# ViT layer with mixture of experts: weight parting, tile list and first gathers moved into the batch stage; own buffer for the second input

## The chip, the cores and the metric

One core of a Trainium2 chip runs the whole layer in one launch. The metric is the device time of that launch in microseconds (us); lower is better. PE is TensorE, ACT ScalarE, DVE VectorE, POOL GpSimd, SP SyncE, which here only issues DMAs.

## The reference, cut to what matters

```
h = attention(x)                           # 8 batches, 512 tokens, width 256, 16 heads
h = concatenate([cls_tok, h], axis=1)      # 513 rows a batch
h = h + ssm(layernorm(h))                  # h_t = W h_(t-1) + B u_t, y = C h + D u
u2 = layernorm(h)
shared = (silu(u2 @ Wg_s.T) * (u2 @ Wu_s.T)) @ Wd_s.T
probs = sigmoid(u2 @ Wr.T + rb); scores, idx = top_k(probs, 2)
out = shared + sum over e of cw[e] * (silu(u2 @ Wg[e].T) * (u2 @ Wu[e].T)) @ Wd[e].T   # 8 experts, inner width 512
return h + out
```

## The kernel before, in words

Four stages follow each other: stage_qkv, stage_attention, stage_mix, stage_experts. Each is a block in which every engine runs its own hand-written list of instructions, with semaphores between the engines. At the end of a block each engine drains and all five meet at a barrier (its rows have the line of the block, L782 for the mix stage, L1350 for the experts, L338 for attention).

**stage_mix** (from L779) goes through the 8 batches in 9 steps: `step(b, par, prev, this, nxt)` does batch b's recurrence (`this`), the shared expert of batch b-1 (`prev`) and the attention output and first normalisation of b+1 (`nxt`). In step b:

- DVE: `normalise(b, ..., 2)` writes the second input into `u`, the same buffer as the first input, `normalise(b + 1, h, 1)` overwrites it. Hence DVE waits for `u2_stored` (SP's store of u to HBM) before the latter (L1252). POOL makes the power (L873) that each `normalise` (L1166) needs. DVE also chooses the two experts of each row (`top_two`), computes their slots (`place`) and at the very end the list of tiles (`list_tiles`, L1324).
- POOL: in `step`, multiplies `ud`, adds `h2`, and scatters 8 times per batch (L900) the row number and weight of each row to its slot in `table` in HBM.
- SP: in `step`, loads the heads of b+1 (L845), loads one expert's weights (L856), stores the second input (L859) and the output rows of b-1 (L863), in that order.
- PE: turns rows by products with `ident` (L981), the recurrence's products (L993, L1049), the shared expert (L1011, L1019). ACT: SiLU and copies of turned tiles.

**Weight parting.** The expert products are exact to FP32 by three short products (`split_products`, L72) of parts: `short` (rounded weight, made by ACT in `shorten_weights`) and `rest` (weight minus short, `cut_weights`). There are 16 places of 128x1024 elements, n = 0 to 7 for wg, 8 to 15 for wu. `rest` lies over the loaded weights, `short` over buffers of the mix stage, so these must be dead first. DVE cuts 11 places (two in step 8, nine in the expert stage), POOL five (three after the last scatters, two after the first gathers). ACT rounds eight in step 8, eight in the expert stage.

**stage_experts** takes 72 tiles of 128 slots in a ring of 8. SP loads a tile's slots (`load_slot`: read the tile's number from `tile_i`, then a DMA), POOL gathers its rows of x (`gather`, L1397), PE turns them (L1434), DVE parts x (L1528, L1530), PE multiplies (L72), turns (L1453) and goes down (L1460), DVE weighs, POOL adds into the output by an indirect DMA (L1407). Before the loop: 8 slot loads, 4 gathers, the last 11 cuts.

The lines that set the order around the change:

```
dve.wait_ge(ev["u2_stored"], 16 * b + 16)          # L1252, ahead of normalise(b + 1, h, 1)
pool.wait_ge(ev["slots_out"], 16 * (2 + 2 * TT * B))   # end of POOL's mix list
pool.wait_ge(mem["acc_stored"], 16 * B)            # experts, ahead of the 4 first gathers
pe.wait_ge(mem["ev_cut"]["dve"], sum(map(len, DVE_CUTS)))
pe.wait_ge(mem["ev_cut"]["pool"], sum(map(len, POOL_CUTS)))   # ahead of the first expert product
```

## Time and profile before

| what | value |
|---|---|
| time, median of 3 runs | 1296.78 us (1296.37 to 1297.04) |
| the profiled execution's own time | 1293.25 us |
| its span, first to last instruction | 1291.2 us, 21179 instructions |
| busy: PE, DVE | 1179.1 us (91%), 832.4 us (64%) |
| busy: ACT, POOL | 496.1 us (38%), 404.7 us (31%) |
| mean granted TensorE clock | 0.962 of full speed |
| mix stage, expert stage | from about 522 to 886, and on to 1291 |

The busy time of an engine is the sum of its instructions' spans. In the timeline views a row gives the start, the duration, the engine (SPq is the queue of SP), the line, the operation with what it writes and reads, how many such instructions follow each other, and in brackets the idle time before it with what ended it. A stretch's row gives busy us and number of instructions per engine, then the granted clock of PE.

### The profile page before, as it was taken

To read this page: it belongs to the slowest core of one execution; us is meant where nothing else is said; L and a number is where in the kernel's file an instruction comes from. 1 tells how busy PE (TensorE), PEld (TensorE's weight loads), DVE (VectorE), ACT (ScalarE), POOL (GpSimd) and SP (SyncE) were. 2 spreads that over 40 slices of the span, in tenths; PEclk is the share of its full clock that TensorE was granted. 3 is DMA by queue.
4 is the path that set the end of the run, shared out by engine and by line. 5 is a ranking of instruction groups with operands and counts; after the bars stand their busy time and mean duration, and the time that the engine had idled before them with its cause. 6 is when DMAs were issued, how large, how long until landed. Compare 5 with 4: busy or idle time off the path is not lost. (4 is left out here: it accounts for less than half of the span.)

```text
span 1291.2 us, 21179 instructions
## 1 busy us (share of the span) xinstructions
PE 1179.1 (91%) x5606; PEld 704.0 (55%) x5607; DVE 832.4 (64%) x1458; ACT 496.1 (38%) x867; POOL 404.7 (31%) x520
## 2 busy tenths in 40 slices
PE   6996999999999999767999999982999999999996
PEld 3652233333333332454566665551888888888885
DVE  4998788888888883367777788856333433333332
ACT  2430777777777778211212121242122222222221
POOL 1021431101101110211444333446344554455443
PEclk9996999999999999878999999996999999999999
DMA  9885233333333321022334323311133333333332
GB/s 287 309 275 184 71 99 93 103 96 96 100 92 97 103 85 34 33 55 77 98 98 97 70 51 75 82 34 33 30 53 49 49 51 55 49 49 49 53 53 33
DMA packets 108674, 113.04 MB, mean 88 GB/s; under 512 B 26080, under 2 KB 97904, under 8 KB 107600
## 3 DMA queue, kind: packets, MB, share of 16 engines
q1 hardware_dynamic: 90528, 89.05, 24.0%
q0 software_dynamic: 18112, 23.57, 10.6%
q8 instruction: 17, 0.28, 0.1%
q14 instruction: 17, 0.14, 0.0%
HBM read 68.81 MB, written 43.62 MB: 87 GB/s over the span
## 5 line engine op out<-in xcount | busy, mean ns | idle before, releaser
L637 DVE TENSOR_REDUCE neg_max<-by_query 128x2 f32<-128x1024 f32 x256 | 301.3, 1219 | 62.5 <-PE by_query L538 61.7
L696 ACT ACTIVATE k_wu_e<-by_key 128x512 f32<-128x512 f32 x512 | 277.2, 600 | 83.5 <-PE by_key L546 80.0
L546 PE MATMUL by_key<-k_wg_e 99*128 99x512 bf16 x512 | 179.2, 384 | 3.8 <-ACT k_wu_e L696 2.1
L538 PE MATMUL by_query<-k_wg_e 96*128 96x512 bf16 x512 | 160.4, 396 | 11.3 <-PEq L106 7.5
L1407 POOL DMA_INDIRECT out_rows<-y,slot x72 | 113.2, 1572 | 182.9 <-DVE y L1544 179.9
L1500 ACT ACTIVATE gate<-ps_up 128x512 f32<-128x512 f32 x72 | 43.2, 600 | 304.4 <-PE ps_up L72 304.4
L1460 PE MATMUL ps_y<-k_wd_e,acts_T 128*128 x576 | 136.1, 379 | 0.8 <-ACT acts_T L1509 0.8
L557 PE MATMUL pv<-k_wu_e,k_wd_e 128*32 128x512 f32 x1024 | 136.2, 604 | 0.2 <-ACT k_wu_e L696 0.2
L546 PEld LDWEIGHTS by_key<-k_wg_e 99*128 99x128 bf16 x512 | 41.9, 97 | 145.3 <-ACT k_wu_e L696 84.6
L1460 PEld LDWEIGHTS ps_y<-k_wd_e,acts_T 128*128 128x128 f32 x576 | 109.1, 190 | 18.6 <-issue 1.0
L1528 DVE CAST x_T<-ps_x 128x256 fp32r<-128x256 f32 x72 | 30.6, 424 | 107.6 <-PE ps_x L1434 107.6
L451 POOL CAST k_max_parts<-neg_max 128x16 bf16<-128x16 f32 x32 | 6.1, 191 | 283.0 <-PE by_key L546 244.8
L538 PEld LDWEIGHTS by_query<-k_wg_e 96*128 96x128 bf16 x512 | 47.2, 99 | 84.6 <-DVE neg_max L637 13.8
L1544 DVE TENSOR_SCALAR y<-ps_y,slot 128x256 f32<-128x256 f32 x72 | 34.8, 483 | 78.0 <-DMA out_rows<-y,slot 51.6
L1397 POOL DMA_INDIRECT x_in<-kept_x_rows,slot x72 | 73.6, 1022 | 31.5 <-issue 21.6
L1537 DVE TENSOR_TENSOR acts<-gate,ps_up 128x512 f32<-128x512 f32 x72 | 49.5, 687 | 52.3 <-PE ps_up L72 52.3
L72 PE MATMUL ps_up<-wg_short,x_T 128*128 x144 | 71.1, 493 | 5.2 <-issue 5.2
L900 POOL DMA_INDIRECT kept_table<-k_pay,k_slot_i x64 | 63.2, 987 | 24.6 <-issue 18.4
L873 POOL TENSOR_TENSOR mix_rstd<-mix_mv,k_minus_half 128x4 f32<-128x4 f32 x16 | 16.4, 1027 | 171.5 <-DVE mix_mv L1161 171.3
L206 PE MATMUL qk_ps<-k_wu_e,k_wqkv 128*128 128x512 f32 x128 | 57.8, 605 | 12.3 <-DMA k_wu_e<-in_xT 12.3
L1011 PE MATMUL mix_pairs<-mix_u_T,k_wg_s 128*128 128x512 f32 x128 | 62.6, 612 | 1.3 <-DVE mix_act_T L1139 1.2
L72 PE MATMUL ps_up<-wu_short,x_T 128*128 x144 | 63.2, 439 | 0.0
(211 smaller groups left out, 1906.8 us busy)
## 6 DMA issues: line engine op xcount, KB each, us to landing
k_wg_e<-kept_qk SPq DMA_DIRECT2D x384, 64.0 KB, 2.2
kept_qk<-qk_parts SPq DMA_DIRECT2D x32, 384.0 KB, 3.4
kept_v<-v_ones SPq DMA_DIRECT2D x8, 1024.0 KB, 5.8
k_wd_e<-kept_v SPq DMA_DIRECT2D x32, 256.0 KB, 3.0
...
```

The source lines that it names most:

```text
L72: mm = pe.matmul(out, short(lhs[a]), short(rhs[b]), start=(start and n == 0), stop=(stop and n == 2))
L206: mm = pe.matmul(qk_ps[:, j, :], wqkv[:, c, j * P:(j + 1) * P], xt[:, par, c, :], start=(c == 0), stop=(c == DC - 1))
L538: pe.matmul(by_query[:, pair_bank(b, g, k // 2) + k % 2, :], q_rows[0:KROWS, g, h, t * P:(t + 1) * P], k_rows[0:KROWS, g, h, :], start=Tru ...
L546: pe.matmul(by_key[:, key_bank(job), :], k_rows[0:SROWS, g, h, kt * P:(kt + 1) * P], q_rows[0:SROWS, g, h, :], start=True, stop=True).then ...
L557: mm = pe.matmul(pv[VW * h:VW * (h + 1), :], v_unit[:, g, kt, h, :], probs[:, G * (kt // 2) + h, kt % 2, :], start=(kt == 0), stop=(kt == ...
L637: dve.tensor_reduce(neg_max[:, g % 2, 2 * n:2 * n + 2], by_query[:, bank:bank + 2, :], AX.X, ALU.max, negate=True).then_inc(query_read, 1)
L696: act.activation(probs[:, key_tile(j) // 2 * G + j // 2 % G, j % 2, :], by_key[:, key_bank(job), :], ACT.Exp, scale=float(HD) ** -0.5).the ...
L900: pool.indirect_dma_start(out=dram["table"], in_offset=None, in_=mem["pay"][:, t, n, :], out_offset=bass.IndirectOffsetOnAxis(ap=mem["slot ...
L1011: mm = pe.matmul(pairs[:, m % 2, n, :], w[:, c, m * P:(m + 1) * P], u2_T[:, c, :], start=(c == 0), stop=(c == DC - 1))
L1397: pool.indirect_dma_start(out=x_in[:, r % X, :], out_offset=None, in_=dram["x_rows"], in_offset=bass.IndirectOffsetOnAxis(ap=slot[:, r % R ...
L1407: pool.indirect_dma_start(out=dram["out"], in_=y[:, r % 2, :], in_offset=None, compute_op=ALU.add, out_offset=bass.IndirectOffsetOnAxis(ap ...
L1460: mm = pe.matmul(ps_y[:, r % 2, 0:D], acts_T[:, m, :], mem["wd_e"][:, bass.ds(e, 1), m, :], start=(m == 0), stop=(m == FC - 1))
```

## The change

1. **Second input in its own buffer.** `normalise(b, ..., 2)` writes `u2`, POOL and the turn of u keep `u`. `normalise(b + 1, h, 1)` waits for the turn of u (`u_turned`) instead of the store; `normalise(b, ..., 2)` waits for u2's turn and store of one batch ago.
2. **Places sorted by last use.** The mix buffers lie in the order in which they die, and `w_short` is one tensor with wg and wu of an expert side by side; place n is now expert n // 2, wg for even n. Places 0 and 1 lie on a piece of their own (`EARLY`).
3. **Parting by ACT and DVE alone.** ACT rounds 0 and 1 before step 0, 2 to 12 in step 7, 13 to 15 in step 8. DVE cuts 0 and 1 in step 0, 2 and 3 in step 7, 4 to 10 in step 8, 11 to 15 in the expert stage. POOL cuts none.
4. **Tile list, slots and gathers in the mix stage.** DVE lists the tiles right after placing the last batch; SP loads 4 slot tiles before the last output store and 4 after it; POOL gathers 4 tiles at the end of its mix list. Two of four scratch buffers of the mix stage (`back`) lie on `x_in`.
5. **SP's order.** An expert's weights are loaded after the store of u2 and for b + 1; expert 0's at the stage's start.

```
+def cut_weights(dve, mem, n):
+    w, rest = ((mem["wg_e"], mem["wg_rest"]), (mem["wu_e"], mem["wu_rest"]))[n % 2]
+    dve.wait_ge(mem["ev_cut"]["shortened"], n + 1)
+    dve.tensor_tensor(short(rest[:, n // 2, :, :]), w[:, n // 2, :, :], mem["w_short"][:, n // 2, n % 2, :, :],
+                      ALU.subtract).then_inc(mem["ev_cut"]["rest_made"], 1)
...
+def load_slot(sp, mem, dram, i, r):
+    q = sp.value_load(mem["tile_i"][0:1, 0, bass.ds(RING * i + r, 1)], min_val=0, max_val=SLOTS // P - 1)
+    sp.dma_start(mem["slot"][:, r, :], dram["table"][bass.ds(q * P, P), :]).then_inc(mem["slot_in"][r], 16)
...
@@ SP, step of the mix stage
                 if this:
-                    for name in ("wg_e", "wu_e", "wd_e"):
-                        sp.dma_start(mem[name][:, bass.ds(b, 1), :, :], dram[name][:, bass.ds(b, 1), :, :]
-                                     ).then_inc(mem["experts_in"], 16)
                     sp.wait_ge(ev["u2_done"], b + 1)
                     sp.dma_start(dram["x_rows"][bass.ds(T1 * b + 1, S), :].rearrange("(t p) n -> p t n", p=P),
-                                 u[:, :, :]).then_inc(ev["u2_stored"], 16)
+                                 u2[:, :, :]).then_inc(ev["u2_stored"], 16)
+                if nxt:
+                    load_expert(b + 1)
+                if not this:
+                    sp.wait_ge(mem["tiles_listed"], 1)
+                    sp.wait_ge(ev["slots_out"], 16 * (2 + 2 * TT * B))
+                    for r in range(FIRST_X):
+                        load_slot(sp, mem, dram, 0, r)
...
+            load_expert(0)
             batches(sp, step)
-            sp.wait_ge(ev["u2_stored"], 16 * B)
+            for r in range(FIRST_X, RING):
+                load_slot(sp, mem, dram, 0, r)
@@ POOL, step of the mix stage
                 if not this:
-                    for n in POOL_CUTS[0]:
-                        cut_weights(pool, mem, n).then_inc(mem["ev_cut"]["pool"], 1)
...
+                    pool.wait_ge(ev["u2_stored"], 16 * B)
+                    pool.wait_ge(ev["cls_stored"], 32)
+                    for r in range(FIRST_X):
+                        pool.wait_ge(mem["slot_in"][r], 16)
+                        pool.sem_inc(ev["scatter_begun"])
+                        gather_x(pool, mem, dram, r)
...
@@ ACT, step of the mix stage
+                if last:
+                    act.wait_ge(mem["experts_in"], 16 * 3 * E)
+                    shorten_weights(act, mem, 2)
+                    act.wait_ge(ev["out_made"], 2 * B)
+                    shorten_weights(act, mem, 3)
...
+                if last:
+                    act.wait_ge(ev["bu_made"], B)
+                    act.wait_ge(ev["ud_done"], 2 * B)
+                    for n in (4, 5, 6):
+                        shorten_weights(act, mem, n)
...
+                if last:
+                    act.wait_ge(ev["state_done"], B)
+                    shorten_weights(act, mem, 7)
+                    act.wait_ge(ev["y_made"], 2 * B)
+                    for n in range(8, 13):
+                        shorten_weights(act, mem, n)
...
@@ DVE, step of the mix stage
                     if not this:
+                        cut_weights(dve, mem, 4)
                         place(b - 1)
                     shared_act(b - 1, 1)
                     if not this:
-                        cut_weights(dve, mem, DVE_CUTS[0][0]).then_inc(mem["ev_cut"]["dve"], 1)
+                        dve.wait_ge(ev["counts_read"], b)
+                        list_tiles(dve, chain(dve, ev["tile_steps"], 0), mem, flat_backs)
+                if not prev:
+                    for n in range(EARLY):
+                        cut_weights(dve, mem, n)
...
                 if this:
+                    dve.wait_ge(ev["u2_turned"], b)
+                    dve.wait_ge(ev["u2_stored"], 16 * b)
                     normalise(b, h2[:, par, :, :], 2)
...
+                if this and not nxt:
+                    for n in (2, 3):
+                        cut_weights(dve, mem, n)
...
                 if nxt:
-                    dve.wait_ge(ev["u2_stored"], 16 * b + 16)
+                    dve.wait_ge(ev["u_turned"], b + 1)
                     normalise(b + 1, h, 1)
@@ experts: PE, DVE
-            pe.wait_ge(mem["ev_cut"]["dve"], sum(map(len, DVE_CUTS)))
-            pe.wait_ge(mem["ev_cut"]["pool"], sum(map(len, POOL_CUTS)))
+            pe.wait_ge(mem["ev_cut"]["rest_made"], 2 * E)
...
-            for n in DVE_CUTS[1]:
-                cut_weights(dve, mem, n).then_inc(mem["ev_cut"]["dve"], 1)
+            for n in range(11, 2 * E):
+                cut_weights(dve, mem, n)
```

How the instructions stand, at three places. First SP at the start of the mix stage and in step 0; `mix_h` and `k_mix_u` are the shared names of the tiles that lie in those places, among them h2 and u2. Before:

```order
L845 DMA k_heads_in<-kept_heads 128x1024 [waits mix_heads_turned,heads_stored]
L852 DMA kept_x_rows<-mix_h 8x256 [waits mix_cls_h2]
L852 DMA out_rows<-k_cls_h 8x256 [waits mix_cls_done]
L856 DMA k_wg_e<-in_wg_e 128x1024
L856 DMA k_wu_e<-in_wu_e 128x1024
L856 DMA k_wd_e<-in_wd_e 128x1024
L859 DMA kept_x_rows<-k_mix_u 128x4x256 [waits mix_u2_done]
```

With the change:

```order
L862 DMA k_wg_e<-in_wg_e 128x1024
L862 DMA k_wu_e<-in_wu_e 128x1024
L862 DMA k_wd_e<-in_wd_e 128x1024
L869 DMA k_heads_in<-kept_heads 128x1024 [waits mix_heads_turned,heads_stored]
L876 DMA kept_x_rows<-mix_h 8x256 [waits mix_cls_h2]
L876 DMA out_rows<-k_cls_h 8x256 [waits mix_cls_done]
L880 DMA kept_x_rows<-k_mix_u 128x4x256 [waits mix_u2_done]
```

Expert 0's loads stand ahead of everything, and the store of u2 (L880) has no weight load ahead of it; expert 1's three follow it.

Second, POOL at the end of the mix stage, from the last eight scatters on. Before:

```order
L900 DMA kept_table<-k_pay,k_slot_i 35072x2 x7
L776 TENSOR_TENSOR wg_rest<-k_wg_e,wg_short 128x1024 [waits weights_shortened]
L776 TENSOR_TENSOR wg_rest<-k_wg_e,wg_short 128x1024 [waits weights_shortened,weights_pool] x2
L782 UNCONDITIONAL_BRANCH [waits mix_slots_out,weights_pool]
L1389 UNCONDITIONAL_BRANCH [waits barrier_Pool_Activation_PE_DVE_SP_gather]
L1397 DMA x_in<-kept_x_rows,slot 128x256 [waits acc_stored,slot_in0]
```

With the change:

```order
L930 DMA kept_table<-k_pay,k_slot_i 35072x2 x7
L791 DMA k_x_in<-kept_x_rows,k_slot 128x256 [waits slot_in0,mix_u2_stored,mix_cls_stored]
L791 DMA k_x_in<-kept_x_rows,k_slot 128x256 [waits slot_in1]
L791 DMA k_x_in<-kept_x_rows,k_slot 128x256 [waits slot_in2]
L791 DMA k_x_in<-kept_x_rows,k_slot 128x256 [waits slot_in3]
L800 UNCONDITIONAL_BRANCH
L1440 UNCONDITIONAL_BRANCH [waits barrier_Pool_Activation_PE_DVE_SP_gather]
```

The four gathers stand ahead of the barrier and in the place of the three cuts.

Third, DVE at the end of the tile list (the last row of it is the cast to k_tile_i). Before:

```order
L1339 TENSOR_REDUCE tile_f<-mix_back 128x72 [waits mix_tile_steps]
L1340 TENSOR_TENSOR tile_f<-tile_f,k_tile_index 128x72 [waits mix_tile_steps]
L1341 CAST k_tile_i<-tile_f 128x144 [waits mix_tile_steps]
L1144 TENSOR_TENSOR mix_h<-mix_pairs,mix_h 128x512 [waits mix_down_made] x2
L782 UNCONDITIONAL_BRANCH
```

With the change:

```order
L1399 TENSOR_REDUCE tile_f<-mix_back 128x72 [waits mix_tile_steps]
L1400 TENSOR_TENSOR tile_f<-tile_f,k_tile_index 128x72 [waits mix_tile_steps]
L1401 CAST k_tile_i<-tile_f 128x144 [waits mix_tile_steps]
L1186 TENSOR_TENSOR mix_act_T<-mix_gate,mix_pairs 128x512 [waits mix_down_made,mix_gate_done]
L778 TENSOR_TENSOR wu_rest<-k_wu_e,w_short 128x1024 [waits weights_shortened]
```

The list stands ahead of the shared expert's last two activations (L1186) and of six of step 8's seven cuts (L778).

## Rows read from the trace of the kernel before

**Rows 1.** Busy time by stretches: us from start, busy us (instructions) per engine

```profile
877.00:904.00 27.00, 1.45 (x5) 0.72 (x5) 16.79 (x19) 7.68 (x8) 14.78 (x8) 0.60 0.15 40
...
955.00:1035.00 80.00, 80.00 (x402) 67.65 (x401) 30.98 (x62) 16.30 (x30) 39.32 (x31) 1.00 0.33 52
```

**Rows 2.** Timeline of PE over the seam: start us, us, engine, line, operation

```profile
869.76 7.17 PE L1019 MATMUL mix_pairs<-k_wd_s,mix_act_T 128*128 128x256 f32 x32 [1.78 <-DVE mix_act_T L1139]
...
897.97 0.66 PE L1434 MATMUL ps_x<-k_ident,x_in 128*128 128x128 f32 x2 [3.19 <-DVE x_rest L1530]
903.87 0.79 PE L72 MATMUL ps_up<-wg_short,x_T 128*128 x1 [5.24 <-issue]
```

**Rows 3.** Timeline of DVE over the seam

```profile
858.90 0.19 DVE L1177 TENSOR_TENSOR k_pos<-mix_turn,k_next_slot 128x32 f32<-128x32 f32 x1 [0.75 <-DMA kept_table<-k_pay,k_slot_i]
...
886.72 3.50 DVE L776 TENSOR_TENSOR wg_rest<-k_wg_e,wg_short 128x1024 fp32r<-128x1024 f32 x3 [4.74 <-PEq L782]
890.13 6.89 DVE L776 TENSOR_TENSOR wu_rest<-k_wu_e,wu_short 128x1024 fp32r<-128x1024 f32 x6
```

**Rows 4.** Timeline of POOL over the seam, and its last DMA of the program

```profile
862.10 0.96 POOL L900 DMA_INDIRECT kept_table<-k_pay,k_slot_i  x1 [6.26 <-DVE k_slot_i L1183]
...
871.51 1.30 POOL L900 DMA_INDIRECT kept_table<-k_pay,k_slot_i  x1 [0.30 <-issue]
...
890.30 1.93 POOL L1397 DMA_INDIRECT x_in<-kept_x_rows,slot  x1 [9.88 <-DMA slot<-kept_table]
892.53 1.92 POOL L1397 DMA_INDIRECT x_in<-kept_x_rows,slot  x1 [0.31 <-issue]
...
897.01 0.94 POOL L1397 DMA_INDIRECT x_in<-kept_x_rows,slot  x1 [0.30 <-issue]
897.97 4.77 POOL L776 TENSOR_TENSOR wu_rest<-k_wu_e,wu_short 128x1024 fp32r<-128x1024 f32 x2
...
1284.87 1.54 POOL L1407 DMA_INDIRECT out_rows<-y,slot  x1 [3.04 <-DMA out_rows<-y,slot]
```

**Rows 5.** One line's instructions: POOL's drains; ns min/median/max, first and last start us

```profile
L782 POOLq DRAIN  x1: 5536/5536/5536, 880.9 to 880.9; - x1
...
L1350 POOLq DRAIN  x1: 6310/6310/6310, 1284.6 to 1284.6; - x1
...
L338 POOLq DRAIN  x1: 3547/3547/3547, 500.4 to 500.4; - x1
```

**Rows 6.** Timeline of DVE in batch 1 and in batch 7

```profile
586.62 1.38 DVE L1166 TENSOR_SCALAR k_mix_u<-k_mix_h,mix_mv,mix_rstd 128x256 f32<-128x256 f32 x4 [7.23 <-DMA kept_x_rows<-k_mix_u]
...
598.04 0.69 DVE L1207 TENSOR_TENSOR mix_back<-mix_made,k_cos 128x512 f32<-128x512 f32 x1 [1.21 <-PE mix_made L1049]
...
818.16 1.38 DVE L1166 TENSOR_SCALAR k_mix_u<-k_mix_h,mix_mv,mix_rstd 128x256 f32<-128x256 f32 x4 [2.06 <-POOL mix_rstd L873]
...
828.12 0.68 DVE L1207 TENSOR_TENSOR mix_back<-mix_made,k_cos 128x512 f32<-128x512 f32 x1
```

**Rows 7.** Timeline of DVE in batch 0, of POOL and PE in batch 1

```profile
549.69 0.69 DVE L1207 TENSOR_TENSOR mix_back<-mix_made,k_cos 128x512 f32<-128x512 f32 x1 [5.67 <-PE mix_made L1049]
...
579.39 1.04 POOL L873 TENSOR_TENSOR mix_rstd<-mix_mv,k_minus_half 128x4 f32<-128x4 f32 x1 [3.67 <-DVE mix_mv L1161]
...
588.14 1.96 PE L981 MATMUL mix_turn<-k_ident,k_mix_u 128*128 128x128 f32 x8 [5.86 <-DVE k_mix_u L1166]
```

**Rows 8.** The scatters' line, window 871 to 872: their landing

```profile
DMA to landing us min/median/max: 3.5/3.9/4.2
```

**Rows 9.** Timeline of SP after the barrier: the eight slot loads

```profile
887.68 8.10 SPq L1379 DMA_DIRECT2D slot<-kept_table  x8
```

**Rows 10.** Timeline of SP and PE in a middle batch: the heads' load and turn

```profile
772.62 0.37 SPq L845 DMA_DIRECT2D k_heads_in<-kept_heads  x1
...
793.00 1.04 PE L981 MATMUL mix_turn<-k_ident,k_heads_in 128*128 128x128 f32 x8
```

**Rows 11.** The line of the expert loads: their landing

```profile
DMA to landing us min/median/max: 4.9/9.8/14.4
```

160 lines of the change are left out of this document (79 added, 81 removed).

## The prediction

> **What bounds the kernel now.** I began with the busy time by stretches [rows 1]. In the tile loop of the expert stage TensorE (PE) is busy all 80.0 of 80 us: no edit outside that loop can help there, and the change leaves its products alone. Between 877 and 904 us, where the batch stage (mix) hands over to the experts, PE is busy 1.45 of 27 us. The timeline of PE tells where that hole lies [rows 2]: the last product of the mix stage begins at 869.76 and lasts 7.17, so it ends at 876.9, and the first expert product starts at 903.87. Then I read the timelines of the engines that PE waits for. POOL scatters the last slots up to 871.51 and then cuts three weight places; DVE restarts at 886.72 after 4.74 us of idleness at the barrier between the stages and cuts nine places, 3.50 and 6.89 us; POOL gathers four tiles from 890.30 on and ends with two cuts, 4.77 us from 897.97, so at 902.7, and PE's first product comes 1.1 us behind [rows 2 to 4]. The barrier's own rows say why it opened at 886.7 though DVE was done at 882: POOL's drain at the end of the stage lasted 5.54 us from 880.9 [rows 5]. Last, the waits in the mix loop: DVE stood 7.23 us before the first-input normalisation of batch 1, for the store of u to land; in the last middle batch the same instruction waits only 2.06, for POOL's power [rows 6].
>
> So two places can give time: batch 0 to 1, and the seam. The page's slices and its total of busy time would not have shown either.
>
> **Batch 0 to 1.** With the second input in u2, the first-input normalisation waits for its POOL power and for PE's turn of the old u, which is long past. The power ran from 579.39 for 1.04 [rows 7], so DVE starts near 580.5 instead of 586.62. PE turned at 588.14 after 5.86 of idleness, so it was free at 582.3 and starts there: 5.9 earlier [rows 7]. Behind it the stretch from this normalisation to the product with cos took 598.04 − 586.62 = 11.4 us in batch 1, with PE cold from the pause, and 828.12 − 818.16 = 10.0 in the later batch [rows 6]. Without the pause I take the 10.0: the product starts at 590.5, 7.5 us earlier. Bounds: 5.9 if PE alone counts, 7.6 at most. Every later batch keeps its rhythm, since there the wait is for POOL: **−7.5 us**, once. The new waits for u2 (turned and stored a batch ago) cost nothing: a whole batch lies between, and even the store of batch 0, the slowest, was over by 586.62, in the middle of the next step.
>
> The two cuts put into batch 0 (2 × 1.15 = 2.3 us on DVE) stand where DVE idles 5.67 us for PE's first product [rows 7]; at twice their length they would still be covered. Their weights are asked for at the stage's start, some 14 us ahead. The two of batch 7 stand where DVE waits for the router product, and ACT's 11 roundings before the last step stand in ACT's waits (ACT is busy 38% of the span). Without cover a cut costs 1.15 us (6.89 for six) [rows 3], a rounding 0.96 (7.68 for eight) [rows 1].
>
> **The seam, step by step, on the clock of the trace before.** (1) The two cuts of batch 7 run beside POOL's scatters. Beside unbroken cuts an indirect DMA took 1.92 to 1.93 us, and 0.94 once the cuts were over, with 0.30 between two [rows 4]. So 2.3 us of cuts cost POOL 2.3 × (1 − 1.24/2.23) = 1.0 us. The last placing began at 858.90, after 0.75 of waiting for scatters to land [rows 3], so it slips by 1.0, to 859.9. The cut that now precedes it ends by then. (2) From the placing to the first scatter: 862.10 − 858.90 = 3.2, so 863.1. The tile list, moved up behind two activations, needs some 5.6 us without POOL's cuts beside it (an estimate: 11.1 us as traced, less three steps held up there), ends near 868.5 and is not what SP waits for last. (3) The eighth scatter began 9.4 us after the first [rows 4]; with four cuts beside them instead of two I add 1.1: it starts at 873.6, and lands up to 4.2 later [rows 8]: 877.8. (4) SP loads a slot tile: 1.0 from release to issue (886.72 to 887.68), then 2.6 to the first gather (890.30) [rows 3, 4, 9]. So the first gather starts at 881.4 and the fourth, three pitches of 1.24 to 1.27 later, at 885.2. The four gathers are now **ahead** of the barrier. (5) POOL must drain behind them. No row shows a drain behind gathers; the nearest is the one at the program's end, behind indirect DMAs: 1284.6 + 6.31 = 1290.9, that is 6.1 after the last one began at 1284.87 [rows 4, 5]. I take it, since it is the only one right behind an indirect DMA: 891.3, and 0.3 to the release, 891.6, which is 4.9 **later** than now. Bounds: 3.55 us behind a plain POOL DMA, or 5.54 as at this place now, counted from the gather's end (886.2 + 5.54 = 891.7) [rows 5]. (6) DVE has five cuts left instead of nine: 5 × 1.15 = 5.75, so 897.3. From the end of DVE's cuts (890.13 + 6.89 = 897.02) to PE's second turn of x it was 0.95 [rows 2, 3]: 898.3. (7) PE loads the expert's number, 1.1 as after POOL's last cut: the first product at 899.4 instead of 903.87: **−4.5 us**.
>
> What was taken off POOL (five cuts) was 1.1 + 4.8 us of the old path at its end; what becomes late next is DVE's five cuts behind a later barrier. The old path's wait for the gathers to land disappears. SP does four slot loads, the last store and four more loads, 1.0 each: done near 888, before POOL's drain. Queued behind SP's wait for the scatters is only that last store, whose sum is made after 877.8 anyway.
>
> The first expert products run at the lower granted clock in both cases, since PE has idled about as long. The rest keeps its pitch: the expert loop has the same number of rows per tile.
>
> A rule speaks to step (1) and (3). The Trainium skill (SBUF — State Buffer, Who interferes with whom) says that a two-input VectorE instruction contends with GpSimd's reads but infers that descriptor writing is left alone, and that a blocked engine blocks fully. The trace disagrees with the first half (1.93 against 0.94 beside just such instructions); by the rule the 2.1 us of delay in my sum would vanish.
>
> Sum: −7.5 − 4.5 = −12.0 us. The profiled execution took 1293.25 (span 1291.2 plus 2.05), 3.5 less than the median 1296.78 of the three runs. On it the sum gives 1281.2; on the median, which I forecast, **1284.8**.
>
> **Rivals.** (a) Scatters and gathers are not held up by cuts: all 2.1 us return, gain 14.1, 1282.7. For: scatters beside single steps of the list kept 0.96 to 1.3. Against: 1.93. Chance 0.12. (b) POOL stands still as long as a cut runs beside it. Then the cuts of batch 7 cost 2.3, not 1.0, and the three or four beside the last scatters cost 3.5, not 1.1: the release comes at 895.3, PE's first product at 903.1, the seam gives 0.8 and the whole 8.3: 1288.5. For: DVE's own steps were held for the whole of a POOL instruction. Chance 0.13. (c) The new wait is met by another in batch 1 (POOL or PE late after all): only the seam's 4.5, 1292.3. Against: nothing else was running. Chance 0.06. (d) **Slower.** SP now issues the three expert loads ahead of the output store and of the next heads. Before, the heads load was issued at 772.62 and turned at 793.00: 20.4 us of room [rows 10]; the weight loads of such a burst land after 9.8 (median) and at most 14.4 [rows 11]. Moved behind three loads of 512 KB, the heads are issued some 1.5 us later and join the burst's end. If they landed over 18.9 us after issue, PE and all behind it would wait, in each of six batches; above 20.9 the 12 us are eaten, at 22 us it is 6 × 3.1 − 12: 6.6 slower, 1303.4. Against: those 14.4. Chance 0.06.
>
> **The numbers.** The forecast has 0.63, the rivals as given. The terms' bounds: 5.9 to 7.6, and for the seam 0.8 (b) to 8.7 (short drain and no hold-up), so 6.7 to 16.3, or 1280.5 to 1290.1; I reach from 1280.0 to 1290.5, which leaves out (c), (d) and something unknown. A measurement tells 0.2% (2.6 us). Faster by more: forecast, (a), (b) and most of (c), 0.91; within: 0.03; slower: 0.06.
>
> **What would show it.** DVE's wait before the normalisation of batch 1 gone and its start near 580.5. Scatters of batches 6 and 7 with some of 1.4 to 1.9 us. Four gathers before the barrier, then a POOL drain of 5 to 6 us, the release near 884 (7.5 earlier than 891.6 on the old clock), five DVE cuts directly after it, and PE's first product near 892. I am wrong if the drain is short (the seam gives more), if the heads wait on a load in the middle batches, or if the tile loop gets longer.

## The result, and the profile after

| | before | changed |
|---|---|---|
| time, median | 1296.57 us (1295.59 to 1297.04, 4 runs) | 1277.3 us (1272.49 to 1280.12, 4 runs) |
| the profiled execution's own time, span | 1293.25, 1291.2 us | 1272.49, 1270.7 us |
| mean granted TensorE clock | 0.962 | 0.969 |
| busy: PE, DVE, POOL | 1179.1, 832.4, 404.7 us | 1168.8, 828.0, 394.5 us |

The ratio is 0.985 (95% interval 0.982 to 0.988): 19.3 us faster, where 12.0 were forecast. 1277.3 lies below the range of 1280.0 to 1290.5. Some of the 19.3 is chance: on the chip of the first experiments the same two kernels had medians of 1292.97 (14 runs) and 1276.89 (5 runs), 16.1 us apart. The first trace is also of the fastest of the four changed runs. The changed kernel was therefore profiled a second time (e1_again below, own time 1277.65); the two traces differ by 5 us at the end, and both are used.

The span, cut at instructions that all three traces have:

| stretch, us | before | changed | changed, again |
|---|---|---|---|
| start to DVE's first-input normalisation of batch 0 | 539.69 | 539.96 | 541.92 |
| on to the product with cos of batch 1 | 58.35 | 47.77 | 51.02 |
| on to that of batch 7 | 230.08 | 227.92 | 227.25 |
| on to the placing of batch 7's slots | 30.78 | 30.32 | 31.10 |
| on to PE's first expert product | 44.97 | 42.71 | 41.35 |
| on to the weighing of tile 66 | 354.05 | 350.11 | 350.92 |
| on to the end | 33.26 | 31.94 | 32.21 |

Against before the first trace gains 10.58, 2.16, 0.46, 2.26, 3.94 and 1.32 after a start 0.27 later; the second gains 7.33, 2.83, −0.32, 3.62, 3.13 and 1.05 after a start 2.23 later. The forecast had 7.5 in the second row, 4.5 in the fourth and fifth together, and nothing elsewhere.

**Batch 0 to 1.** DVE's timeline of the changed kernel; it answers to [rows 6]:

```profile
577.61 1.38 DVE L1214 TENSOR_SCALAR k_mix_u<-k_mix_h,mix_mv,mix_rstd 128x256 f32<-128x256 f32 x4 [1.14 <-POOL mix_rstd L903]
...
587.73 0.68 DVE L1260 TENSOR_TENSOR k_x_in<-mix_made,k_cos 128x512 f32<-128x512 f32 x1
```

The wait of 7.23 us for the store is gone; what is left is 1.14 for POOL's power. The start is even earlier than POOL's power at 579.39 + 1.04 allowed [rows 7], because all of batch 0 was quicker. PE's timeline says why. The changed kernel:

```profile
544.54 3.70 PE L1096 MATMUL mix_made<-k_mix_u_T,k_m_T 128*128 128x512 f32 x8 [2.04 <-ACT k_mix_u_T L963]
...
557.29 5.69 PE L1040 MATMUL mix_made<-k_m_T,k_mix_hidden 128*128 128x256 f32 x16 [6.46 <-DVE k_mix_hidden L1276]
```

The same program, profiled again:

```profile
546.49 5.39 PE L1096 MATMUL mix_made<-k_mix_u_T,k_m_T 128*128 128x512 f32 x8 [2.04 <-ACT k_mix_u_T L963]
...
560.81 6.76 PE L1040 MATMUL mix_made<-k_m_T,k_mix_hidden 128*128 128x256 f32 x16 [6.33 <-DVE k_mix_hidden L1276]
```

Same products, same idle time ahead (2.04 us), 3.70 us against 5.39. It is the granted clock. It has two levels in these traces, 1.00 (2.4 GHz) and 0.5 (1.2 GHz); the value of a stretch is a mean of the two. Rows of busy time by stretches (us busy and instructions of PE, granted clock, DMA share, GB/s), first the changed kernel, then its second profile at the same instructions, then before:

```profile
545.00:560.00 15.00, 8.54 (x30) 0.82 0.00 1
560.00:575.00 15.00, 10.08 (x45) 0.84 0.18 49
```

```profile
547.00:562.00 15.00, 8.67 (x27) 0.73 0.00 1
562.00:577.00 15.00, 10.08 (x30) 0.61 0.01 2
```

```profile
545.00:560.00 15.00, 8.67 (x27) 0.73 0.00 1
560.00:575.00 15.00, 10.18 (x30) 0.61 0.04 5
```

The second profile has before's clock and is the fair comparison: 7.3 us gained. The other 3.25 of the first profile are clock in batch 0 that one execution gets and another does not. There is a pair at the higher clock too: r2_before_merged below, which is the kernel before with every byte at its old address, took 55.27 there (clock 0.86 from 545 to 560 us, 0.80 from 560 to 575), and the change took 47.77, 7.5 less. So the gain is the same at either clock. The Trainium skill (TensorE: Matmul & The Clock Gate, What's actually happening) says that the ramp is "run-variable"; the two traces of the changed kernel agree.

**Middle batches.** From one product with cos to the next, batches 3 to 5 took 38.4 us each before and 37.7 with the change. POOL's timeline in batch 4, before:

```profile
704.44 2.36 POOL L879 TENSOR_TENSOR k_mix_ud<-k_mix_u,k_d_row 128x1024 f32<-128x1024 f32 x1 [1.50 <-DVE k_mix_u L1166]
707.02 2.35 POOL L885 TENSOR_TENSOR mix_h<-k_mix_ud,k_mix_h 128x1024 f32<-128x1024 f32 x1 [0.23 <-POOL k_mix_ud L879]
```

DVE's timeline there; these steps on 128x32 elements take 0.19 us elsewhere:

```profile
704.49 2.35 DVE L734 TENSOR_TENSOR k_eq<-mix_probs,k_best 128x32 f32<-128x32 f32 x1
...
707.09 2.33 DVE L736 TENSOR_TENSOR k_key<-k_eq,k_iota_e 128x32 f32<-128x32 f32 x1
```

POOL with the change:

```profile
694.03 2.35 POOL L909 TENSOR_TENSOR k_mix_ud<-k_mix_u,k_d_row 128x1024 f32<-128x1024 f32 x1 [1.50 <-DVE k_mix_u L1214]
700.18 2.41 POOL L915 TENSOR_TENSOR mix_h<-k_mix_ud,k_mix_h 128x1024 f32<-128x1024 f32 x1 [3.80 <-DMA out_rows<-mix_h]
```

The second POOL instruction now waits 3.80 us for the output store of batch 2 to land, and thereby comes when DVE is through with its small steps: only one of them is blocked. The store lands late since SP's expert loads now stand ahead of it. From issue to landing, in that batch, before and after:

```profile
DMA to landing us min/median/max: 7.0/7.0/7.0
```

```profile
DMA to landing us min/median/max: 14.2/14.2/14.2
```

Where the same wait was short, nothing was gained: the first two output stores landed after 11.3 us, the addition behind them waited 0.99 and 0.98 us (first trace), and batches 1 and 2 kept 38.31 and 38.19 us. The Trainium skill (SBUF — State Buffer, Who interferes with whom) has a rule for such a block: a VectorE instruction with two SBUF inputs contends with a GpSimd one that reads SBUF, and the contention is an exclusive lock. The rows agree: 2.33 to 2.35 beside POOL's 2.35. That a step held up by 2.15 us costs a batch only some 0.7 is measured, not explained.

**The seam.** POOL's timeline with the change; it answers to [rows 4]:

```profile
849.17 1.16 POOL L930 DMA_INDIRECT kept_table<-k_pay,k_slot_i  x1 [5.14 <-DVE k_slot_i L1231]
...
861.18 1.92 POOL L930 DMA_INDIRECT kept_table<-k_pay,k_slot_i  x1 [0.30 <-issue]
870.12 1.00 POOL L791 DMA_INDIRECT k_x_in<-kept_x_rows,k_slot  x1 [7.02 <-DMA k_slot<-kept_table]
...
873.95 0.94 POOL L791 DMA_INDIRECT k_x_in<-kept_x_rows,k_slot  x1 [0.30 <-issue]
```

POOL's drain at the end of the stage, as in [rows 5], then DVE and PE behind the barrier, as in [rows 2, 3]:

```profile
L800 POOLq DRAIN  x1: 7652/7652/7652, 873.0 to 873.0; - x1
```

```profile
880.95 1.23 DVE L778 TENSOR_TENSOR wu_rest<-k_wu_e,w_short 128x1024 fp32r<-128x1024 f32 x1 [16.36 <-PEq L800]
```

```profile
887.66 0.66 PE L1477 MATMUL ps_x<-k_ident,k_x_in 128*128 128x128 f32 x2 [5.90 <-DVE x_rest L1569]
888.68 0.79 PE L72 MATMUL ps_up<-w_short,x_T 128*128 x1 [0.36 <-issue]
```

Gathers ahead of the barrier, a drain that ends 6.7 us after the last gather's start (873.0 + 7.65 = 880.65), DVE idle for 16.4 us and then five cuts on the path: the forecast's picture, most pieces a little longer.

The first scatters show something that the forecast did not count: the tile list, moved up, runs beside them. In the first trace its step on 128x264 elements starts just ahead of the first scatter (1.16 us, in the block above), in the second just behind it:

```profile
849.07 0.43 DVE L1388 TENSOR_TENSOR k_x_in<-counts,k_tile_rows 128x264 f32<-128x264 f32 x1
```

```profile
854.50 0.96 POOL L930 DMA_INDIRECT kept_table<-k_pay,k_slot_i  x1 [5.34 <-DVE k_slot_i L1231]
854.64 0.43 DVE L1388 TENSOR_TENSOR k_x_in<-counts,k_tile_rows 128x264 f32<-128x264 f32 x1
```

The first four scatters took 1.16, 1.37, 1.51 and 1.02 us in the first trace, 0.96, 0.96, 0.96 and 1.32 in the second.

**The tile loop.** PE's timeline inside one tile, before:

```profile
1009.23 0.39 PE L72 MATMUL ps_up<-wg_short,x_rest 128*128 x1
1009.46 0.40 PE L72 MATMUL ps_up<-wg_short,x_T 128*128 x1
1009.70 0.39 PE L72 MATMUL ps_up<-wg_rest,x_T 128*128 x1
```

And with the change:

```profile
991.72 0.39 PE L72 MATMUL ps_up<-w_short,x_rest 128*128 x1
991.95 0.39 PE L72 MATMUL ps_up<-w_short,x_T 128*128 x1
992.17 0.39 PE L72 MATMUL ps_up<-wg_rest,x_T 128*128 x1
```

The starts stand 0.235 us apart before ((1009.70 − 1009.23) / 2) and 0.225 with the change, both at the full granted clock. This triple shows more than the mean: between 960 and 1240 us the starts within a run of six such products stand 0.2333 us apart on average before (first gap left out) and 0.2294 in both changed traces. Over 60 tiles the pitch, the time from one tile to the next, is 5.188 us before and 5.151 and 5.154 with the change: 2.0 to 2.2 us.

### The profile page after: what moved, and what is told of

Same layout as the page of the kernel before. It is cut to its first block and busy times, and to the rows that moved or that the text cites. A ratio compares the mean times of both kernels' runs of the same rounds, so it can differ in the third digit from the quotient of the medians.

```text
span 1270.7 us, 21184 instructions
## 1 busy us (share of the span) xinstructions
PE 1168.8 (92%) x5606; PEld 699.3 (55%) x5607; DVE 828.0 (65%) x1463; ACT 496.1 (39%) x867; POOL 394.5 (31%) x515
## 3 DMA queue, kind: packets, MB, share of 16 engines
q0 software_dynamic: 18112, 23.57, 10.7%
## 5 line engine op out<-in xcount | busy, mean ns | idle before, releaser
L1455 POOL DMA_INDIRECT out_rows<-y,k_slot x72 | 113.9, 1583 | 189.8 <-DVE y L1583 175.2
L538 PE MATMUL by_query<-k_wg_e 96*128 96x512 bf16 x512 | 161.3, 398 | 11.6 <-PEq L106 7.5
L72 PE MATMUL ps_up<-w_short,x_T 128*128 x288 | 133.5, 464 | 0.4 <-issue 0.4
L72 PE MATMUL ps_up<-w_short,x_rest 128*128 x288 | 113.8, 395 | 0.0
L1583 DVE TENSOR_SCALAR y<-ps_y,k_slot 128x256 f32<-128x256 f32 x72 | 34.8, 484 | 77.9 <-DMA out_rows<-y,k_slot 64.1
L791 POOL DMA_INDIRECT k_x_in<-kept_x_rows,k_slot x72 | 70.7, 982 | 28.7 <-issue 21.1
L930 POOL DMA_INDIRECT kept_table<-k_pay,k_slot_i x64 | 67.1, 1049 | 23.5 <-issue 18.4
L903 POOL TENSOR_TENSOR mix_rstd<-mix_mv,k_minus_half 128x4 f32<-128x4 f32 x16 | 16.4, 1026 | 149.3 <-DVE mix_mv L1208 149.2
L1058 PE MATMUL mix_pairs<-k_mix_u_T,k_wg_s 128*128 128x512 f32 x128 | 61.3, 602 | 0.7 <-DVE mix_act_T L1186 0.6
## 6 DMA issues: line engine op xcount, KB each, us to landing
k_heads_in<-kept_heads SPq DMA_DIRECT2D x8, 512.0 KB, 11.3
```

The lines of the kernel that those rows point to most:

```text
L72: mm = pe.matmul(out, short(lhs[a]), short(rhs[b]), start=(start and n == 0), stop=(stop and n == 2))
L538: pe.matmul(by_query[:, pair_bank(b, g, k // 2) + k % 2, :], q_rows[0:KROWS, g, h, t * P:(t + 1) * P], k_rows[0:KROWS, g, h, :], start=Tru ...
L791: pool.indirect_dma_start(out=mem["x_in"][:, r % FIRST_X, :], out_offset=None, in_=dram["x_rows"], in_offset=bass.IndirectOffsetOnAxis(ap= ...
L930: pool.indirect_dma_start(out=dram["table"], in_offset=None, in_=mem["pay"][:, t, n, :], out_offset=bass.IndirectOffsetOnAxis(ap=mem["slot ...
L1058: mm = pe.matmul(pairs[:, m % 2, n, :], w[:, c, m * P:(m + 1) * P], u2_T[:, c, :], start=(c == 0), stop=(c == DC - 1))
L1455: pool.indirect_dma_start(out=dram["out"], in_=y[:, r % 2, :], in_offset=None, compute_op=ALU.add, out_offset=bass.IndirectOffsetOnAxis(ap ...
```

## The experiments

All ratios are to the kernel before, run on the same chip. "Batch 0 to 1" is the second row of the table above, 58.35 before and 51.02 at the same clock with the change.

### The changed kernel again

> The changed kernel, unaltered, to see which of its gains come back and why its runs spread over 7.6 us where the kernel before spreads over 1.5. Theory A (the gains are in the order of the work): again a normalisation of batch 1 near 577.6, middle batches 3 to 6 at 37.7 us each against 38.4, POOL's drain of 7 to 8 us, first expert product 15 us earlier, tile pitch 5.147 against 5.187; the spread comes from a stretch that differs between executions. Theory B (some of it was chance): TensorE's granted clock between 545 and 575 us is back at 0.6 to 0.7, the normalisation of batch 1 comes near 580, and the tile pitch is 5.187 again; the time is then 3 to 6 us longer, about 1277.

Measured: median 1276.89 (1275.45 to 1277.65), ratio 0.987 (0.985 to 0.989). Clock of batch 0 at 0.73 and 0.61, as B had it; middle batches 37.65 to 37.79, drain 6.94, tile pitch 5.154, first product 11.2 us earlier instead of 15. So the pitch and the batches behind batch 1 are the program's, the 3.25 us are chance. The kernel before spread too on this chip, 1290.06 to 1297.38 over 14 runs: its narrow range of 1.5 us was that of four runs.

### Is it the buffer or the order of the DMAs?

b1_order_only, in the kernel before:

```
+                    sp.wait_ge(ev["u2_done"], b + 1)
+                    sp.dma_start(... u[:, :, :]).then_inc(ev["u2_stored"], 16)
                     for name in ("wg_e", "wu_e", "wd_e"): ...
-                    sp.wait_ge(ev["u2_done"], b + 1)
-                    sp.dma_start(... u[:, :, :]).then_inc(ev["u2_stored"], 16)
```

> The kernel before, with one edit: an expert's three weight loads are issued behind the store of the second input instead of ahead of it. Theory O (the order of SP's DMAs set the wait of 7.23 us): the store of batch 0 is issued 1.4 us earlier and lands in 4 to 6 us instead of 11.6, before 580.5; the normalisation of batch 1 starts near 580.5 as with the change, and the time falls by 7 to 8 us to about 1289, with the one buffer. Theory U (the own buffer is what removes the wait, as the prediction had it): the store still lands after 584 and the gain is under 3 us.

e2_store_wait_back, in the changed kernel: `+ dve.wait_ge(ev["u2_stored"], 16 * b + 16)` ahead of `normalise(b + 1, h, 1)`.

> The changed kernel, with the old wait put back: the first-input normalisation of b+1 waits again for the store of the second input of b. Theory O (SP's order did it): the store of batch 0 landed at 577.20 in the changed kernel, 0.4 before that normalisation, so nothing moves by more than 0.5 us and the time stays within 2 us of the changed kernel. Theory U (the own buffer did it): the normalisation of batch 1 is 6 us later and so is the end, about 1283.

e3_buffer_only, in the changed kernel: `if nxt: load_expert(b + 1)` moved from behind the store of u2 to ahead of it.

> The changed kernel, with the expert loads of b+1 again issued ahead of the store of the second input (expert 0 stays at the start). Theory S (late landing of the output store is what shortened the middle batches: it landed 13 to 14.6 us after issue instead of 7, so POOL's addition of h slid from right behind ud to 4 us later, out from under DVE's choice of experts, which it had blocked for 2.35 us): the output store lands after about 7 us again, POOL's addition stands again at once behind ud, DVE has two blocked steps of 2.35 us per batch, batches 3 to 6 take 38.3 each again and the end is 2 to 3 us later; the normalisation of batch 1 stays where it is. Rival: the middle batches are shorter for another reason (clock, placing of buffers): they stay at 37.7.

| | batch 0 to 1 | batches 3 to 5, each | median | ratio |
|---|---|---|---|---|
| before | 58.35 | 38.4 | | |
| order only (b1) | 51.00 | 37.6 to 37.9 | 1288.78 | 0.996 (0.995 to 0.998) |
| buffer only (e3) | 51.08 | 38.2 to 38.4 | 1276.68 | 0.987 (0.985 to 0.990) |
| both, waits as before (e2) | 47.87 | 37.6 to 37.8 | 1273.81 | 0.986 (0.984 to 0.988) |
| both (e1) | 51.02 | 37.7 to 37.8 | 1276.89 | 0.987 (0.985 to 0.989) |

(b1, e3 and e1 had the lower clock in batch 0, e2 the higher, like the first trace.) Either edit alone removes the wait: with the order alone the store has no weight load ahead of it and lands in 6.0 us instead of 11.6, in time. Theory O is right, as e2 says too (the store's wait is back in the changed kernel and costs nothing), and the forecast's "with the second input in u2" named a sufficient cause, not the only one. b1 ended only 4 to 5 us ahead of before, less than the two columns give. Its trace shows where that went: in the kernel before, the loads of expert 7 are issued in step 7, now behind the store and so amid the last scatters, the last four of which took 6.7 to 8.4 us from start to landing instead of 3.9 to 4.4; DVE's placing of batch 7 waited 5.28 us for them, where it waited 0.75 [rows 3]. The change loads expert 7 a batch earlier and has no such burst. Theory S holds for e3: POOL's addition stood at once behind ud again (idle 0.23), and the middle batches were long again, in the buffer's presence; in b1 they were short without it. The medians of e1 and e3 do not tell 2 to 3 us apart; the traces do.

h1_add_later, in the kernel before: `+ pool.wait_ge(ev["chosen_done"], b)` ahead of POOL's addition.

> The kernel before, with one wait more: POOL's addition of h (h2 = ud + h) of batch b waits until DVE has chosen the experts of batch b-1. Theory S (what shortened the middle batches is that this addition no longer blocks one of DVE's small steps for 2.35 us; the order of SP's DMAs only brought it about): the addition slides by about 3.5 us, the second blocked step is gone, and batches 3 to 6 take 37.6 to 37.8 us instead of 38.4; batches 1 to 6 give 3 to 4 us in all, about 1290. Rival (the order of SP's DMAs shortens them in another way, such as PE's or DVE's reads beside the transfers): they stay at 38.4.

Measured: 1290.4, ratio 0.997 (0.996 to 0.999). POOL:

```profile
704.47 2.35 POOL L879 TENSOR_TENSOR k_mix_ud<-k_mix_u,k_d_row 128x1024 f32<-128x1024 f32 x1 [1.50 <-DVE k_mix_u L1167]
710.04 2.42 POOL L886 TENSOR_TENSOR mix_h<-k_mix_ud,k_mix_h 128x1024 f32<-128x1024 f32 x1 [3.22 <-DVE mix_chosen L1197]
```

Batches 1 to 6 took 37.6 to 37.9, 3.8 us less in all, with SP's order untouched. A wait of 3.2 us was **added** and the kernel got faster: the block was the cause, the late store only its accident.

### The seam

c1_all_cuts_early: the last loop of cuts moves from the expert stage to the end of DVE's mix list.

```
+                    if not this:
+                        for n in range(11, 2 * E):
+                            cut_weights(dve, mem, n)
...
-            for n in range(11, 2 * E):
-                cut_weights(dve, mem, n)
```

> The changed kernel, with the last five cuts moved from the expert stage to the end of DVE's list in the mix stage, where DVE idles 16 us for the barrier. Theory D (from the barrier on, DVE's five cuts of 5.75 us and nothing else set the first expert product; the barrier waits for POOL's drain alone): the cuts run from 864 to 870, ahead of the gathers, the barrier opens where it did, the first product comes 5.0 to 5.8 us sooner behind the barrier (2 to 3 us instead of 7.9), and the time falls by 5 to 6 us to about 1271. Rival L (the first product would then wait for something else: the loaded expert number, the landing of x, or the cuts hold up the last scatters and with them the barrier): under 3 us.

g1_gathers_behind: POOL's four gathers stand at the start of its expert list.

> The changed kernel, with the four first gathers behind the barrier again (slots are still loaded ahead of it). Theory Q (POOL's drain waits for the gathers' work and costs 6.7 us from the last gather's start): the drain starts behind the last scatter, near 866, takes 5 to 6 us and ends long before SP has issued its last slot load at 878, so the barrier opens near 880 instead of 884.8 (clock of the second run of the changed kernel); the gathers then run beside DVE's five cuts, two of them at 1.9 us, and the first product comes 2 to 4 us earlier. Rival M (the gathers ahead of the barrier are a gain, as the prediction had it): the first product comes 2 to 4 us later.

c2_cuts_early_rest_behind: both, and SP's slot loads 4 to 7 at the start of its expert list.

> The changed kernel with three moves: the last five cuts at the end of DVE's mix list, the four first gathers behind the barrier, and the slot loads of tiles 4 to 7 behind it too. Theory D+Q (with the two edits run apart, POOL's drain ended 6.9 us after the last scatter's start, SP's last load held the barrier, and DVE's cuts held PE): now the barrier opens when SP has issued the four slot loads and the output store, about 0.4 us after that store, near 25 us behind the placing of the last batch (34.9 in the changed kernel); the gathers run with no cut beside them at 0.95 us each, the first lands 4 us after its start, and the first expert product comes 31 to 33 us after that placing instead of 41.4 to 42.7, so 9 to 11 us sooner: about 1266. Rival P (POOL's drain or the landing of the gathers takes what the cuts gave): 36 us or more, a gain under 6.

c4_two_slots_first: as c2, SP issues the last output store first and only two slot loads ahead of the barrier.

> The kernel of the run before it, and SP issues the last output store ahead of the slot loads and only two slot loads ahead of the barrier. Theory Q (what opens the barrier is the later of POOL's drain, 6.9 us after the last scatter's start, and SP's last issue): POOL's drain decides, the barrier opens 1.5 to 2 us sooner, the first product 1 to 2 us sooner, the time 1 to 2 us below that kernel's. Rival: the first gather must wait for slots and x to land whenever the barrier opens, and the gain is under 0.5 us.

| | placing to barrier's opening | placing to first product | median | ratio |
|---|---|---|---|---|
| changed (e1) | 33.4 | 41.35 | 1276.89 | 0.987 (0.985 to 0.989) |
| c1 | 35.1 | 38.28 | 1274.44 | 0.983 (0.980 to 0.985) |
| g1 | 30.0 | 37.95 | 1273.44 | 0.983 (0.980 to 0.985) |
| c2 | 26.3 | 32.98 | 1269.4 | 0.981 (0.978 to 0.984) |
| c4 | 26.5 | 33.26 | 1267.71 | 0.979 (0.976 to 0.982) |

(The opening is the end of the last drain: POOL's in e1 and c1, SP's in g1 and c2, DVE's in c4.) The change's own seam is not one number: from placing to first product it took 41.35 to 43.28 us in the eight traces that left it alone, and e1's is the shortest, so against the others each gain below is up to 1.9 larger. Theory D half fell in c1: behind the barrier only 3.2 us were left instead of 8.0, as it said, but the cuts ended 26.0 us behind the placing, not 24.0 as expected; PE's last products ran at the lower clock and DVE waited for them. The cuts ran beside two gathers (1.18 and 1.92 us), and the barrier opened later than in e1. The first product came 3.1 us earlier than in e1 where 5.0 to 5.8 were expected. In g1 POOL's drain ended at 869.3, 6.9 us after the last scatter's start, and SP's last slot load, issued at 876, held the barrier; two of the gathers ran beside cuts at 1.92 and 1.95, and still it gained 3.4. In c2 all three obstacles are gone. PE there:

```profile
879.10 0.66 PE L1478 MATMUL ps_x<-k_ident,k_x_in 128*128 128x128 f32 x2 [12.36 <-DMA k_x_in<-kept_x_rows,k_slot]
880.83 0.66 PE L1478 MATMUL ps_x<-k_ident,k_x_in 128*128 128x128 f32 x2 [1.07 <-DVE x_rest L1570]
881.83 0.79 PE L72 MATMUL ps_up<-w_short,x_T 128*128 x1 [0.34 <-issue]
```

What it waits for is now the gathers' landing. The 32.98 lie in the expected 31 to 33; the gain is 8.4 us against e1 and 9.7 against the first trace (9 to 11 expected), and the median stayed above the expected 1266. c4 gave nothing there, where 1 to 2 us were expected: with PE's last products at the lower clock, DVE's cuts ended at 877.0 and opened the barrier, not SP. Its median and c2's cannot be told apart.

### The pitch of a tile

p1_before_64 and p2_after_64: `+ sb("pad", [P, 16], FP32)` ahead of the weight buffers, in the kernel before and in the changed one.

> The kernel before, with 64 bytes of nothing ahead of the weight buffers, so that they start at 50432 instead of 50368 bytes (a multiple of 128). Nothing else is altered. Theory G (the tile loop of the changed kernel is 0.036 to 0.04 us a tile shorter because the weight buffers now start at multiples of 128 bytes): the products of 512 columns stand 0.227 to 0.230 us apart instead of 0.233, the tile pitch is about 5.15 instead of 5.19, 2.5 us in all. Rival R (the register arithmetic for the address of the merged short tensor, or its interleaved layout, does it): the pitch stays 5.187 to 5.194.

> The changed kernel, with the same 64 bytes ahead of the weight buffers, so that they start at 54592 instead of 54528 bytes and no longer at a multiple of 128. Theory G (alignment): the tile pitch goes from 5.152 to about 5.19, 2.5 us in all. Rival R (register arithmetic or layout): it stays 5.15.

r1_flat_view and r2_before_merged:

```
-                                        (w_short[:, bass.ds(e, 1), which, c, :], rest...
+                                        (flat_short[:, bass.ds(2 * e + which, 1), c, :], rest...
```

```
-            for name in ("wg_rest", "wu_rest", "wg_short", "wu_short"): ...
+            for name in ("wg_rest", "wu_rest"): ...
+            both = later.enter_context(nc.sbuf_tensor("w_short", [P, 2, E, DC, F], FP32))
+            mem["wg_short"], mem["wu_short"] = both[:, 0, :, :, :], both[:, 1, :, :, :]
```

> The changed kernel, in which PE names the merged short weights as one row of 16 places, 2e + which, instead of expert e and half: the same bytes at the same addresses, another register arithmetic on TensorE's queue. Theory V (the 0.036 us a tile in the expert loop come from that arithmetic, which the merged tensor altered): the pitch of a tile moves off 5.152, toward 5.19. Theory Y (they come from how the weights lie, the two halves of an expert side by side): the pitch stays 5.15.

> The kernel before, with the two short tensors as halves of one (all of wg, then all of wu): every byte at its old address, only the tensor and with it PE's address arithmetic altered. Theory V (arithmetic): the pitch of a tile leaves 5.187, toward 5.15. Theory Y (layout): it stays at 5.185 to 5.194.

| | pitch of a tile, us | ratio |
|---|---|---|
| before; p1; r2 | 5.188; 5.184; 5.187 | 1; 0.999 (0.998 to 1.001); 1.001 (1.000 to 1.003) |
| changed; p2; r1 | 5.151 and 5.154; 5.157; 5.153 | 0.985 and 0.987; 0.987 (0.984 to 0.989); 0.989 (0.987 to 0.992) |

Alignment to 128 bytes fell as the cause of the 0.036. In r2 the register instructions of TensorE's queue changed in kind (from 960 to 1240 us 282 plain ones instead of 390, 619 fused instead of 511) and the pitch did not. That is half of the way to the changed kernel's 172 and 724, so it speaks against arithmetic without closing it; r1 tells little, since its queue stayed as it was. What is left, by elimination and not by a run that shows it, is how the weights lie, which the change altered in two ways at once (the halves of an expert side by side, and `x_in` and `slot` ahead of all). In p2 the same 64 bytes did move the spacing, from 0.2294 to 0.2305 us. Which of the two ways it is, and why it costs some 0.003 us a product, stays open: the order of the places is bound to when the mix buffers die, so the one could not be altered without the other here.

### The clock in batch 0

w1_warm, in the changed kernel, w2_warm_best on c2:

```
+            def keep_warm(to, n):
+                for _ in range(n):
+                    pe.matmul(to, ident[:, :], mem["wg_s"][:, 0, :], start=True, stop=True)
...
+                    if not prev:
+                        keep_warm(made[:, 0, :], 4)
                     pe.wait_ge(ev["uT_copied"], b + 1)
...
+                    if not prev:
+                        keep_warm(cls_ps[1][:, 0:S], 14)
                     pe.wait_ge(ev["state_done"], b + 1)
...
+                    if not prev:
+                        keep_warm(cls_ps[1][:, 0:S], 10)
                     pe.wait_ge(ev["u2_done"], b + 1)
```

> The changed kernel, in which TensorE fills its waits of step 0 (2.0, 6.4 and 4.9 us) with 4, 14 and 10 products of 256 columns whose result nobody reads. Theory K (the spread of its runs comes from batch 0, where the product with m1 took 3.70 us in one execution and 5.39 in another behind the same wait of 2.04 us): the product takes 3.7, the y products 3.7 instead of 5.7 or 6.8, the product with cos of batch 1 comes 62 to 64 us behind the stage's first instruction instead of 64.6 to 68.2, runs spread over less than 4 us, and the median falls by 3 to 5 us. Rival (the clock falls whatever TensorE does, or DVE and POOL set the path of batch 0 anyway): no less than 64.6 us, the same spread.

> The kernel with the last five cuts in the mix stage and gathers and slot loads 4 to 7 behind the barrier, and TensorE's waits of step 0 filled as in w1_warm. Theory K: 2 to 4 us below the same kernel without the filling, about 1265. Rival: the same 1269 as without.

The idle products turned out to have 512 columns, not 256, and took twice the time meant: 12.18 us where 6.4 were free. The clock stayed at 1.00, but the y products came 6.5 us late. Medians 1280.54 and 1271.19, no better than without. Yet the spreads were 2.9 and 1.3 us, so the theory was tried again with half the filling (2, 6, 5): w3_warm_half on the changed kernel, w4_warm_half_best on c2, and w5_all, which is w4 with the wait of h1_add_later.

> The changed kernel, with TensorE's waits of step 0 filled by 2, 6 and 5 idle products of 512 columns, 0.90 us each at full clock as w1_warm showed: 1.8, 5.4 and 4.5 us, which fit into waits of 2.0, 6.4 and 4.9. Theory K (the clock in batch 0 makes the spread): granted clock 1.00 from 545 to 580, product with m1 3.6, both sets of products after it 3.6; the product with cos of batch 1 comes 62 to 64 us behind the stage's first instruction, the median is 1272 to 1275 and the spread under 3 us. Rival: the clock still falls in the short gaps that are left, with a spread over 5 us and 1276 to 1278.

> The same filling on the version with the last five cuts in the mix stage and gathers and slot loads 4 to 7 behind the barrier. Theory K: 5 to 6 us below the long filling on that version (1271.2), so 1265 to 1266, with a spread under 3 us. Rival: 1268 to 1270, like the version without filling.

> The version before it, with POOL's addition of h waiting for the choice of experts as well. Theory S: batches 3 to 7 are as they were, since the late output store already held the addition back there; batches 1 and 2 lose their blocked step and take 37.6 to 37.9 instead of 38.2 to 38.5, so 0.6 to 1.2 us in all. Rival: nothing, under 0.3 us.

PE in w3_warm_half, and its clock in the windows shown above:

```profile
544.66 3.70 PE L1102 MATMUL mix_made<-k_mix_u_T,k_m_T 128*128 128x512 f32 x8 [0.32 <-ACT k_mix_u_T L963]
...
557.41 3.72 PE L1044 MATMUL mix_made<-k_m_T,k_mix_hidden 128*128 128x256 f32 x16 [1.30 <-DVE k_mix_hidden L1286]
```

```profile
545.00:560.00 15.00, 13.70 (x48) 1.00 0.01 2
560.00:575.00 15.00, 14.09 (x62) 1.00 0.31 77
```

| | batch 0 to 1 | median (range) | ratio |
|---|---|---|---|
| w3 | 44.41 | 1271.77 (1269.59 to 1273.8) | 0.983 (0.980 to 0.986) |
| w4 | 44.43 | 1263.24 (1261.96 to 1267.7) | 0.976 (0.974 to 0.979) |
| w5 | 43.78 | 1259.4 (1258.48 to 1262.13) | 0.973 (0.971 to 0.976) |

Theory K is right on the time (3.4 us below the better of the two clocks in batch 0, 6.6 below the other) and wrong on the spread: 4.2 and 5.7 us where under 3 was expected. Part of the rest lies ahead of the mix stage, where batch 0 starts anywhere from 539.7 to 543.4 us over the profiled executions, and part in the last batches: in 18 of the 20 traces the granted clock fell to the lower level for a while between 820 and 866 us, at other instants each time. Neither was followed up. In w5 batches 1 and 2 took 37.72 and 37.65, as theory S had it, against 38.30 and 38.20, and all six gave 1.15 us. The medians of w4 and w5 lie 3.8 us apart; the other 2.7 are not the wait's: in the profiled executions w5 also started batch 0 1.45 us earlier and took 2.1 less from batch 7's product with cos to its placing, where w4 had the lower clock twice. At 1259.4 us **w5 is the fastest version**, 2.7% under the kernel before and 1.2 points beyond the change.

## Why the prediction was wrong in size

Two steps failed, both terms put at nothing: "The rest keeps its pitch", where the repeat at equal clock gave 4.2 us (the first trace 5.3), and "Every later batch keeps its rhythm", where it gave 2.8 (2.2). The seam was over-rated by 1.2 to 1.8.

**Batch 0 to 1, −7.5: right.** At equal clock it measured −7.33 (lower) and −7.5 (higher). In the first trace another 3.25 came from the clock, which the forecast took as fixed ("with PE cold from the pause"). The pause was gone, as it said; that the products of batch 0 run at either clock from run to run was not in the one trace of before.

**SP's order (rival d) had the wrong sign.** The rival saw that three loads now stand ahead of the heads and the output store, and asked only when the heads would be late. They landed after 11.3 us (median) instead of 7.0, and nobody waited. The store landed after 13 to 14.6, and POOL did wait for it. The step that failed is "Every later batch keeps its rhythm, since there the wait is for POOL": its premise was true, but POOL's addition held DVE as well as being waited for. The two rows of 2.33 and 2.35 us on DVE were to be seen before; the forecast used such rows only for rival (b). Worth 2.2 to 2.8 us.

**The seam, −4.5: measured −2.7 and −3.3.** By its own steps, in us behind the placing of batch 7:

| step | predicted | changed | again |
|---|---|---|---|
| first scatter | 3.2 | 3.2 | 3.2 |
| eighth scatter | 13.7 | 15.2 | 13.4 |
| first gather | 21.5 | 24.2 | 22.7 |
| fourth gather | 25.3 | 28.0 | 26.7 |
| DVE's first cut behind the barrier | 31.7 | 35.0 | 33.7 |
| first product | 39.5 | 42.7 | 41.4 |

Three terms were too small, and one too large:

- First to eighth scatter: 10.5 predicted, 12.0 and 10.2 measured. Step (3) added only the cuts; the list, which the change moved from 10.7 us behind the placing to 3, runs beside the first four scatters. In 13 of the 15 traces with the list there its first step began 2.9 us behind the placing, the first scatter took 1.16 or 1.17 and the eight 12.0 to 12.1; in e1 and c4 it began 3.16 behind, the first scatter took 0.95 or 0.96 and the eight 10.2. The clock alone does not decide it: in e1 and r1 it fell at the same place ahead of the placing (829.8 and 830.1 us), and r1 took 12.0.
- Eighth scatter to first gather: 7.8 predicted, 8.9 and 9.3 measured. The landing was taken from [rows 8], 4.2 behind a scatter of 1.30; behind scatters of 1.92 and 1.97 it came after 4.7 and 5.1. In the five other traces with gathers ahead of the barrier and an eighth scatter of 0.95 or 0.96 this stretch took 7.9 to 8.4.
- The drain: 6.1 from the last gather's start (the row that it rests on gives 6.04), 6.7 measured in both, and 6.7 in every other run with gathers ahead of the barrier; behind the end of the indirect DMA it is 5.8 here and was 4.5 at the program's end, for a reason that no run shows.
- The slip of the placing, the other way: it was put at 1.0 and was 0.3 in the second trace; this stretch varied from 30.0 to 32.1 us over four traces of programs whose batch 7 and seam are the old ones (before, p1, r2, h1), so the 0.3 says little.

Barrier to product fitted to 0.1: 7.8 predicted, 7.7 measured.

From placing to product alone, old seams took 44.8 to 45.1 us in five traces and the change's 41.35 to 43.28 in eight, so 1.5 to 3.8 gained where the forecast had 5.5. One bound of the forecast does not come out of its terms: 4.5, 2.1 for no hold-up and 1.6 for the short drain are 8.2, not 8.7; it changes nothing here.

**Holding up by cuts (steps 1 and 3, against rival a): right in kind.** Beside unbroken cuts scatters and gathers took 1.92 to 1.98 us, alone 0.94 to 0.96. Rival (b), a full block, did not show.

**"The rest keeps its pitch": wrong.** The expert stage gave 3.1 to 3.9 us and the tail 1.1 to 1.3. Of it 2.1 are the products of the tile loop, 0.003 us closer each, about 1 the first tiles, where PE stood for gathers ([rows 2] show only the seam; before, the third weighing came 6.03 us after the second instead of 5.19, with the change 5.21), and some 0.5 a stall in the last eight tiles that was gone. The two stalls are not the program's: p2, the changed kernel with 64 bytes more, had both again (6.15 and 5.94 us), and p1 had little of either (5.40 and 5.50). So 2.1 us repeat, and their cause is open; the rest is a matter of one execution. The forecast counted rows of a tile, not their spacing.

So the named mechanisms gave 10.6 at equal clock where 12.0 were forecast, and the places that the forecast had at zero gave another 7.0 from the start of batch 0 on. The signs named for the forecast nearly came true in the second trace (DVE's cuts from 884.95, first product at 892.64, against 884 and 892), and that was luck: batch 0 started 2.2 us later and the seam gave 1.2 less, while the middle batches gave 2.8 more.
